# Mixer: when the first norm's statistics are taken, and when x is weighed by the decay

## What is computed

```python
h = _layernorm(x) * (1 + ca) + sa                 # the first norm
zxbcdt = h @ in_proj_w.T
z, xBC, dt = split(zxbcdt)
dt = softplus(dt + dt_bias)
xBC = silu(conv4(xBC) + conv_b)                   # causal, 4 taps, by channel
xs, Bm, Cm = split(xBC)
dA = exp(-dt * exp(A_log))
# per token: state = state * dA + dt * x * B ;  y = state . C
y = y + D * xs
y = y * silu(z)
y = y * rsqrt(mean(y * y) + EPS) * norm_w
x = x + ga * (h + y @ out_proj_w.T)
h = _layernorm(x) * (1 + cb) + sb                 # the second norm
```

## Time and profile before

| | us |
|---|---|
| median of three runs | 643.15 |
| lowest, highest | 638.3, 648.62 |
| the profiled execution | 639.96 |
| its span in the profile | 638.0 |
| PE busy in the span | 546.5 (86%) |
| DVE busy | 444.5 (70%) |
| ACT busy | 360.4 (56%) |
| POOL busy | 267.7 (42%) |

### The profile page before, as it was taken

How to read it: one execution, slowest core, us unless ns; L and a number is a source line. 1 busy time by engine, 2 the same in 40 slices (tenths; PEclk the granted TensorE clock), 3 DMA queues, 4 the chain that set the end, 5 groups by cost and what they waited for, 6 DMA issues and landing times.

```text
span 638.0 us, 13876 instructions
## 1 busy us (share of the span) xinstructions
PE 546.5 (86%) x3457; PEld 452.1 (71%) x3457; DVE 444.5 (70%) x1657; ACT 360.4 (56%) x1013; POOL 267.7 (42%) x324
## 2 busy tenths in 40 slices
PE   5588888898998989978789999973599999999593
PEld 3467677776777877766467877763599999999441
DVE  3746868577776657768568999997366666666267
ACT  4767584848485674834446656641266556666234
POOL 2213323241314123322102666677266666676333
PEclk9889999889998789989989999995699999999797
DMA  9399999990000000000064111111222222222383
GB/s 271 115 256 172 182 179 186 172 188 19 0 18 1 2 17 2 17 1 17 18 173 142 44 36 44 40 39 56 56 66 72 66 74 69 69 69 65 111 210 100
DMA packets 76395, 54.78 MB, mean 86 GB/s; under 512 B 10524, under 2 KB 69408, under 8 KB 76184
## 3 DMA queue, kind: packets, MB, share of 16 engines
q1 hardware_dynamic: 70352, 43.39, 33.9%
q0 software_dynamic: 4320, 8.99, 4.2%
q10 hardware_dynamic: 1640, 1.45, 0.7%
HBM read 40.62 MB, written 31.58 MB: 113 GB/s over the span
## 4 chain that ended last, share of the span: by engine, by line
PE 40%; issue 34%; DVE 11%; POOL 10%; DMA 4%; ACT 1%; ACTq 1%; POOLq 0%; SPq 0%; DVEq 0%
PE bank L1852 11%; PE bank L1870 10%; PE bank L1722 3%; PE bank L1738 3%; POOL arena L279 2%; PE bank L1728 2%; POOL arena L291 1%; POOL queue L1277 1%; DMA arena<-in_conv_w 1%; PE bank L1843 1%; POOL arena L267 1%; POOL x L297 1%; PE bank L1713 1%; POOL arena L294 1%; DVE nmx L1485 1%
## 5 line engine op out<-in xcount | busy, mean ns | idle before, releaser
L284 POOL TENSOR_TENSOR arena<-arena,half_neg 128x1 f32<-128x1 f32 x32 | 17.6, 550 | 196.0 <-ACT arena L442 196.0
L1317 POOL DMA_INDIRECT results<-arena x71 | 75.7, 1067 | 55.0 <-ACT arena L1416 50.4
L1852 PE MATMUL bank<-front,arena 128*128 128x128 f32 x568 | 78.5, 282 | 1.1 <-issue 0.3
L1870 PE MATMUL bank<-h_all,front 128*128 x568 | 75.5, 276 | 0.1
L1277 POOL DMA_INDIRECT queue<-arena,pos x64 | 63.1, 985 | 28.5 <-issue 13.8
L1852 PEld LDWEIGHTS bank<-front,arena 128*128 128x128 f32 x568 | 70.6, 195 | 4.3 <-issue 3.1
L1870 PEld LDWEIGHTS bank<-h_all,front 128*128 128x128 f32 x568 | 69.4, 193 | 0.3 <-issue 0.3
L1635 DVE COPY arena<-arena 128x516 f32 x71 | 35.9, 506 | 42.5 <-PE bank L1852 34.6
L684 PE MATMUL bank<-h_hi,wc_hi 128*128 128x512 f32 x96 | 46.6, 486 | 15.5 <-ACT arena L436 15.5
L1410 ACT ACTIVATE front<-bank 128x128 f32<-128x128 f32 x71 | 19.7, 278 | 53.6 <-PE bank L1843 52.7
L1648 DVE TENSOR_SCALAR front<-bank,arena 128x128 f32<-128x128 f32 x142 | 42.8, 342 | 4.7 <-PE bank L1852 4.5
(11 more groups left out here) (282 smaller groups left out, 1498.1 us busy)
## 6 DMA issues: line engine op xcount, KB each, us to landing
queue<-in_pad_rows SPq DMA_DIRECT2D x8, 2178.0 KB, 33.1
arena<-queue SPq DMA_DIRECT2D x71, 66.0 KB, 1.9
rows<-mod_rows SPq DMA_DIRECT2D x8, 384.0 KB, 6.3
x_keep<-x SPq DMA_DIRECT2D x8, 256.0 KB, 2.3
arena<-in_w SPq DMA_DIRECT2D x1, 2048.0 KB, 8.8
h_all<-in_w SPq DMA_DIRECT2D x1, 2048.0 KB, 8.6
h_all<-results SPq DMA_DIRECT2D x8, 256.0 KB, 4.8
arena<-results SPq DMA_DIRECT2D x8, 256.0 KB, 5.1
```

The lines of the kernel that those rows point to most:

```text
L1317: pool.indirect_dma_start(k.results, bass.IndirectOffsetOnAxis(ap=xg[:, c, D:D + 1].bitcast(I32), axis=0), yw[:, c, :], None).then_inc(S[f ...
L1852: mm = t_.matmul(bank[(2 if g < NG // 2 else 6) + p][:, g * P:g * P + P], wc[:, p, g * P:g * P + P], xt[:, p, :], start=True, stop=True)
L1870: mm = t_.matmul(bank[4 + p][:, 0:D], ht[:, p, g * P:g * P + P], w2[:, e, g, :], start=(g == 0), stop=(g == NG - 1))
```

## The change

Two edits. In ScalarE's program the four weighings become a function, called at the old place in the first and third slot, and in the second slot behind the silu of line 436 (439 in the new numbering). In VectorE's program the statistics, aggregates and the addition of eps for sequences gl = 3 to 7 move from the third slot (c = 2) to the first two: two chunks in the first slot, two in the second, where the addition of eps now stands too. For gl = 0, 1, 2 all stays in the third slot. POOL's power for them stays at the end of its third slot, and line 521 at the head of VectorE's fourth.

```diff
--- before.py
+++ after.py
@@ -407,12 +407,15 @@
                 if front and c == 0:
                     z_leaves(f, 2)
                     z_leaves(f, 3)
-                if chunk(s) and c < 3:
+                def weigh_x():
                     wait(act, "s_xdt", s + 1)
                     wait(act, "s_lt", s + 1)
                     for h in range(NH):
                         ac.activation(xdw[:, s % 2, h * HD:h * HD + HD], xdt[:, s % 2, h * HD:h * HD + HD], ACT.Copy,
                                       scale=lt[:, s % 2, h * P + P - 1:h * P + P]).then_inc(S["s_xdw"], 1)
+
+                if chunk(s) and c in (0, 2):
+                    weigh_x()
                 if front and c == 1:
                     wait(act, "d_dax", f + 1)
                     act.wait_ge(S["set_pool"], 1)
@@ -434,6 +437,8 @@
                     if f == 1:
                         wait(act, "w_lo", NTAP + 2)
                     ac.activation(xc[:, f % 2, c, :], bank[n % 2][:], ACT.Silu, bias=conv_b[:, c:c + 1]).then_inc(S["f_ev"], 1)
+                if chunk(s) and c == 1:
+                    weigh_x()
                 t = s - 1
                 if chunk(t):
                     wait(act, "s_yz", t + 1)
@@ -595,10 +600,11 @@
                         wait(dve, "s_ymm", t + 1)
                         wait(dve, "f_ev", ring["z", tb, 3] + 1)
                         v.tensor_tensor(yz[:, t % 2, 0:DI], bank[5][:, 0:DI], zs[:, tb % 2, tc, :], ALU.mult).then_inc(S["s_yz"], 1)
-                if gl < NB and c == 2:
+                norm = ({2: (0, 1, 2, 3)} if gl < 3 else {0: (0, 1), 1: (2, 3)}).get(c, ()) if gl < NB else ()
+                if norm:
                     wait(dve, "x_in0" if gl == 0 else "x_in1" if gl == 1 else "x_in2", 16)
                     wait(dve, "l1_ag", NC * gl)
-                    for i in range(NC):
+                    for i in norm:
                         v.bn_stats(st1[:, i, :], x[:, gl * NC + i, :]).then_inc(S["l1_st"], 1)
                 if chunk(s) and c == 0:
                     wait(dve, "o_w", seventh["cum", b] + 1)
@@ -624,16 +630,16 @@
                     else:
                         wait(dve, "o_x", s - 1)
                         dve.nop(nofuse=True).then_inc(S["o_r"], 1)
-                if gl < NB and c == 2:
-                    wait(dve, "l1_st", NC * (gl + 1))
-                    for i in range(NC):
+                if norm:
+                    wait(dve, "l1_st", NC * gl + norm[-1] + 1)
+                    for i in norm:
                         v.bn_aggr(mv1[:, i, :], st1[:, i, :]).then_inc(S["l1_ag"], 1)
                 t = s - 2
                 if chunk(t):
                     wait(dve, "o_x", t + 1)
                     wait(dve, "l2_ag", t)
                     v.bn_stats(st2[:], x[:, t, :]).then_inc(S["l2_st"], 1)
-                if gl < NB and c == 2:
+                if norm and norm[-1] == NC - 1:
                     wait(dve, "l1_ag", NC * (gl + 1))
                     wait(dve, "l1_rs", gl)
                     v.tensor_scalar(ve1[:], mv1[:].rearrange("p c t -> p (c t)")[:, 1::2], EPS, None, ALU.add).then_inc(S["l1_ve"], 1)
```

## The result

The kernel before took 648.5 us (median of 20 executions, 638.3 to 655.2), the changed one 652.7 us (20 executions, 643.3 to 661.5). The ratio is 1.012 (95% interval 1.0075 to 1.017): slower by 1.2%, some 5 to 11 us. Over all executions the means are 646.8 and 653.1 us: 6.3 us slower, with a standard error of 1.3. On another chip the same kernel gave a ratio of 1.019 (1.012 to 1.026) and a mean 5.5 us (standard error 1.8) over the kernel before. I had forecast 644 us in a range of 637 to 651. The time is above the range, and the change cost some 6 us in the mean (4 by the medians, 8 by the ratio) where I had summed 2.0.

What follows compares the result with a forecast made beforehand. TensorE was taken to bound the mixer, busy 237.45 of 269 us. Second slots (+0.5 us) and fourth slots (+1.5) summed to +2.0 on a base of 642.5: 644.5, rounded down to 644, range 637 to 651.

Steps and rivals of the forecast that it cites:

- The weighing worth 0.29 us instead of 1.07: Second slot: moving 1.07 us of weighing behind the silu gains only 0.29, since the exp still waits for line 651.
- Sequence 6 gives nothing: Sequence 6: moving the weighing changes nothing there, as the silu is waited for only in sequences 0 to 5.
- First slot: Two statistics ahead of line 607 delay TensorE's projection by 0.43 us; it reaches the second slot's projection 0.22 late.
- absorbed: Lower bound for the second slot's exp: 0 us later if the first slot's delay is absorbed.
- Second slot: Line 651 comes 0.57 us late, the exp 0.2 later (bounds 0 and 0.3): +0.8 us over sequences 1 to 4.
- nothing late: Second slot of sequence 0: no output work there, so nothing late to wait for and 0 us change.
- Third and fourth slot: Line 294 stretches from 1.09 to 1.55 us, so lines 304 and 521 come 0.30 late: +1.5 us over five sequences.
- The sum: Whole kernel: +0.5 us from the second slots and +1.5 from the fourth slots, +2.0 us in all.
- The base: Time of the kernel before, taken as 642.5 us, the average of four executions, to which the +2.0 was added.
- Rival B: Mixer: longer TensorE waits drop the two sequences at clock 1.00 to the slower pace, +7.8 us, 652; chance 0.12.
- slow stretches that vanish by luck: Mixer clock moving the other way, sequence 4 back to 33.3 us (-3.9), some 640 us in all; chance 0.08.
- my bounds of 0.91 to 0.97: Sign: the prediction is wrong if the granted clock in the mixer leaves 0.91 to 0.97.

Runs made afterwards that it cites:

- e1: Kernel before with only the weighing moved behind the second slot's silu, statistics left in the third slot: 636.7 us, ratio 0.998 to before.
- g1: Changed kernel with POOL's line 304 moved to the second slot and the exp's input (line 651) moved earlier on VectorE: 631.7 us, ratio 0.986 to before.
- g3: Same as g1, with all statistics also placed behind VectorE's copy of line 607: 631.8 us, ratio 0.985 to before.
- f3: Changed kernel with VectorE's subtraction of line 663 moved forward in the third slot, away from POOL's line 294: 635.8 us, ratio 1.006 to before.
- e3: Changed kernel with POOL's power of line 304 for sequences 3 to 7 moved to the end of its second slot: 628.1 us, ratio 0.992 to before.
- f0: Changed kernel run again unaltered, beside the kernel before on the same chip: 643.7 us, ratio 1.019 to before.
- h2: Changed kernel with 4 matmuls that nobody reads ahead of the fourth slot's output projection only: 631.2 us, ratio 0.995 to before.
- h1: Changed kernel with 7 matmuls that nobody reads ahead of the third slot's convolution only: 637.0 us, ratio 1.002 to before.

## Why the prediction was wrong, point by point

**The weighing worth 0.29 us instead of 1.07: right.** e1 gives 0.30 a sequence and a silu wait of 1.48, and the exp follows line 651. "Sequence 6 gives nothing" was wrong: it loses 0.66. I had looked at its silu wait and not at what the weighing delays.

**First slot: half right.** The wait for line 607 grew, but I compared with the 0.45 of one sequence; sequence 1 of before already had 0.81 (109.31 us), with the clock at 1.00 throughout. Between sequences 0 and 1, both at full clock, it went from 0.45 to 0.83, as forecast (0.88). It cost nothing in the period: g1 and g3 differ in this and have one period. Of the bounds that I had named, "absorbed" was the true one.

**Second slot: mis-sized.** The forecast was 0.2 us later for the exp, and it came 0.17 earlier (silu wait 1.78 to 1.61). From line 618 to the end of line 651 VectorE took 0.98 us before (188.94 to 189.92). Now it takes 1.10 (196.83 to 197.93): 0.12 more for two aggregates and line 639, not 0.35, since they fit among the short instructions there. The 0.22 from the first slot doesn't show. Line 639 itself, taken at 0.17 from the earlier trace rows, measured 0.15. In sequence 0 "nothing late" failed in the profiled execution: at a low clock ScalarE waited 1.17 us for line 657.

**Third and fourth slot: right.** Line 294 took 1.53 to 1.55 us in each such slot (forecast 1.55), line 304 came at once behind it, TensorE's wait went from 0.75 to 1.05 (forecast 1.05) four times and in sequence 0 from 1.05 to 1.32. f3 and e3 show the cause by taking it away. The Trainium skill, GPSIMD Engine Reference, section Key points, names contention of GpSimd with VectorE instructions that have two SBUF inputs; these runs agree, with 1.10 us for line 294 where line 663 was moved away and 1.55 where it was not.

**The sum: near, but by luck.** At one clock the changed kernel costs +1.9 us (standard error 0.4) against my +2.0. The terms behind it don't agree so well. The rows give +1.5 for the fourth slots, -0.7 for the silu wait of sequences 1 to 4 (forecast +0.8), -0.3 for sequence 5 and +0.66 for sequence 6 (forecast 0), together +1.2, and sequence 1's period is some 0.2 shorter besides. The rest of the +1.9 has no row that I can name.

**The steps that failed: the base and the clock.** The forecast of 644 missed 652.7 by 8.7 us: 6.0 of it is the base, 0.5 the rounding down, and the rest, 2.2, is what the medians moved beyond the summed 2.0 (4.3 beyond it by the means).

*The base* put the time outside the range. I took the mean of four executions, 642.5 us; the median of twenty is 648.5. The executions of before lie between 638 and 655, with a standard deviation of 4.4, so four of them don't fix the median within less than about 5 us. Set on 648.5, my range would have been 643 to 657 and would have held the result. It should have been wider upward for that alone.

*The clock* is the term of the change that was missing. Rival B had the mechanism, its place (the longer fourth-slot wait) and two sequences falling to a slower pace (in the profile 1 and 3, by 2.7 and 3.5 us, where B said 0 and 1 by 3.9). I gave it 0.12 and left its price out of the sum. That its 652 is the measured time is luck, since it stood on the base of 642.5. The wrong step was to treat the clock as luck that can go either way ("slow stretches that vanish by luck", 0.08). The earlier trace rows already had sequences with the same work at 1.00 and at 0.86, so this kernel sits where a little decides. In such a place 0.3 us more idle in a wait next to a fall is no coin toss. Over 23 executions of before and 6 of the changed kernel the mean clock went from 0.930 to 0.923, which is +3.5 us on top of the +1.9 (f0), and from 0.933 to 0.922, +5.2 us, for the statistics alone; each of the two has a standard error of 1.4 us. One of my own signs said so: the mixer's granted clock (40 to 309 us) left my bounds of 0.91 to 0.97 in the first profile, with 0.89, though f0's profile has 0.94 as before. h2 shows it from the other side: filling that wait and nothing else gives back 12 us, which is more than the change had lost, since before has slow stretches too.

The Trainium skill, TensorE: Matmul & The Clock Gate, section What's actually happening, puts the cost of the clock's ramp at under 1% of a typical kernel's span. That is one ramp at a kernel's start; here the clock falls again and again in mid-kernel, and the changed kernel (643.7) and h2 (631.2), which differ by the filling of 0.9 us of idle a sequence, lie 2% apart, on two chips.

**What stays open.** Why the clock falls in one sequence and not in the next with the same work isn't settled, nor is why the short stretch comes around the silu wait. How the clock part divides between the two waits isn't either, since h1 and h2 were run only beside before, not beside the changed kernel. The 11 us behind the mixer in the changed kernel's first profile have no cause in the change that I can see. Chips differ as well: at a clock of 0.93 the changed kernel's mean is 650.3 us in the first result and 640.4 in f0. A filling of the fourth slot on top of g1 wasn't tried.

## What to carry to other kernels

Before costing an edit by the waits on its path, look at whether stages with the same work stand at different granted clocks; if they do, price every lengthened wait of TensorE by what one more slow stretch costs (here 2.7 to 3.0 us each, beside 0.3 us of wait), times the share of sequences in which it may come, and put it into the sum. An operation that an edit frees gives nothing until the next one in line is moved as well: find that second holder (here line 651 behind line 618, line 304 behind line 294) and move it in the same step, which turned +1.2% into -1.5% (ratios of different blocks). And take the base from as many executions as can be had, or widen the range by their scatter: here the base alone, 6.0 us off, was what the range didn't hold.

## What the chip showed that I had not expected

TensorE work that nobody reads made the kernel faster: 4 small matmuls (1.03 us of passes) in each fourth slot raised the mean granted clock from 0.923 to 0.946 and took the time from 643.7 to 631.2 us, with the period at full clock unchanged at 33.0 (medians of two chips; against the means of their own befores the two stand 12 us apart). A matmul of 128x96 in f32 appears as two passes: 4 as x8 in 1.03 us, 12 as x24 in 2.82 us, which is why the first filling outlasted the wait of 1.8 us by a microsecond. And one VectorE instruction of 0.69 us beside it stretched POOL's line 294 by 0.45 us, from 1.10 to 1.55.
